# All loops of a hybrid block written out, and six PSUM banks shared three and three in its decayed attention

## The reference, cut to what matters

```python
x = x + mamba_block(_layernorm(x))        # stage "m"
x = x + local_attention_ffn(_layernorm(x))  # stage "t0", 2 layers
x = x + decayed_attention(_layernorm(x))  # stage "a"
x = x + local_attention_ffn(_layernorm(x))  # stage "t1", the same 2 layers
```

```python
qkv = x @ Wqkv_w.T + Wqkv_b                  # 16 heads of 8 columns
scores = einsum('bhsd,bhtd->bhst', q, k) / sqrt(8)
decay = exp(-abs(distance_decay[0]) * abs(s - t))
attn = softmax(scores * decay, axis=-1)      # over all 512 positions
out = einsum('bhst,bhtd->bhsd', attn, v)
return out @ out_w.T + out_b
```

## Time and profile before

| | |
|---|---|
| median of 3 runs (lowest to highest) | 2450.01 us (2449.64 to 2451.04) |
| profiled execution, its own time | 2449.7 us |
| its span | 2447.9 us |
| share of the span: PE, PEld, DVE, ACT, POOL | 90%, 61%, 67%, 61%, 69% |
| mean granted clock of PE | 0.96 of full speed |
| stage m | about 0 to 300 us |
| stage t0: local attention, feed-forward, for each layer | 300 to 605, 605 to 678; 678 to 965, 965 to 1045 |
| stage a, the decayed attention | 1045 to 1700 |
| stage t1, as t0 | 1700 to 2005, 2005 to 2080; 2080 to 2370, 2370 to 2448 |

### The profile page before, as it was taken

How to read it: one execution, slowest core, us unless ns; L and a number is a source line. 1 busy time by engine, 2 the same in 40 slices (tenths; PEclk the granted TensorE clock), 3 DMA queues, 4 the chain that set the end, 5 groups by cost and what they waited for, 6 DMA issues and landing times.

```text
span 2447.9 us, 60289 instructions
## 1 busy us (share of the span) xinstructions
PE 2202.7 (90%) x19744; PEld 1500.7 (61%) x19760; DVE 1628.1 (67%) x3905; ACT 1487.5 (61%) x4130; POOL 1679.2 (69%) x1712
## 2 busy tenths in 40 slices
PE   6998799998989998949998889998999979999989
PEld 4776467775657775525555555554677755677755
DVE  5777578875567775636665566666788755677755
ACT  3555378886378886325554455554788853788853
POOL 6777699884188884247665667665899831888842
PEclk8999899999999998979999999999999999999999
DMA  4000011121111111121101110110111211111111
GB/s 108 1 0 1 6 39 31 27 46 28 41 43 36 36 34 26 36 61 53 43 21 41 52 46 20 38 52 17 29 37 28 46 23 46 41 36 33 35 28 49
DMA packets 121250, 86.69 MB, mean 35 GB/s; under 512 B 85560, under 2 KB 102160, under 8 KB 118800
## 3 DMA queue, kind: packets, MB, share of 16 engines
q1 hardware_dynamic: 119248, 82.70, 14.1%
q10 hardware_dynamic: 1856, 2.23, 0.3%
HBM read 30.38 MB, written 8.39 MB: 16 GB/s over the span
## 4 chain that ended last, share of the span: by engine, by line
PE 50%; DVE 12%; POOL 9%; issue 8%; DMA 5%; SPq 3%; ACT 1%; DVEq 0%; POOLq 0%
PE bank L1170 8%; POOL store L1010 6%; PE bank L519 6%; PE bank L638 5%; PE bank L1161 4%; PE bank L1181 4%; DMA store<-parts 4%; PE bank L553 3%; PE bank L566 3%; PE bank L592 3%; PE bank L647 3%; PE bank L533 3%; DVE store L842 2%; POOL store L1019 2%; DVE store L847 2%
## 5 line engine op out<-in xcount | busy, mean ns | idle before, releaser
L1398 POOL TENSOR_SCALAR store<-store 128x512 f32<-128x512 f32 x512 | 349.8, 697 | 217.9 <-DVE store L1315 216.2
L1272 ACT ACTIVATE store<-bank 128x512 f32<-128x512 f32 x512 | 285.9, 604 | 316.4 <-PE bank L1170 315.6
L1315 DVE CUSTOM_DVE_ANT_0 store<-bank,store 128x512 f32<-128x512 f32 x512 | 340.2, 689 | 189.4 <-PE bank L1161 118.9
L730 ACT ACTIVATE store<-bank,store 128x128 f32<-128x128 f32 x1024 | 364.2, 378 | 68.6 <-DVE store L860 68.5
L1010 POOL TENSOR_TENSOR store<-store 128x16 f32<-128x16 f32 x128 | 372.6, 2911 | 26.4 <-DVE store L856 26.4
L1004 POOL TENSOR_TENSOR store<-store 128x512 f32<-128x512 f32 x256 | 321.2, 1276 | 83.3 <-DVE store L847 82.0
L1170 PEld LDWEIGHTS bank<-store 128*128 128x128 f32 x2048 | 252.4, 147 | 136.3 <-ACT store L1272 78.3
L1170 PE MATMUL bank<-store 128*128 128x128 f32 x2048 | 309.7, 285 | 0.0
L519 PE MATMUL bank<-store 128*128 128x512 f32 x512 | 268.8, 612 | 8.5 <-DVE store L835 7.0
L1019 POOL TENSOR_TENSOR store<-store 128x512 f32<-128x512 f32 x256 | 261.6, 1043 | 17.4 <-POOL store L1010 11.4
L1161 PE MATMUL bank<-store 72*128 72x512 bf16 x512 | 186.6, 397 | 86.1 <-DMA store<-parts 46.8
(11 more groups left out here) (199 smaller groups left out, 4457.7 us busy)
## 6 DMA issues: line engine op xcount, KB each, us to landing
store<-store SPq DMA_DIRECT2D x256, 128.0 KB, 2.3
store<-parts SPq DMA_DIRECT2D x96, 192.0 KB
parts<-store SPq DMA_DIRECT2D x16, 384.0 KB, 2.5
store<-store SPq DMA_DIRECT2D x128, 32.0 KB
store<-store SPq DMA_DIRECT2D x128, 31.8 KB
store<-store SPq DMA_DIRECT2D x32, 127.0 KB
store<-in_L_ffn_wqkv_dram SPq DMA_DIRECT2D x4, 768.0 KB, 4.5
out_dram<-store SPq DMA_DIRECT2D x8, 256.0 KB, 2.6
```

The lines of the kernel that those rows point to most:

```text
L730: last = nc.scalar.activation(prob[:, e, b, :], bank[3 + e][:, b * P:(b + 1) * P], ACT.Exp, bias=nmax[:, e, b:b + 1], accum_out=psums[:, h ...
L1272: nc.scalar.activation(AT[:, h % 4, c, :], bank[2 + c][:, :], ACT.Exp, scale=-1.0).then_inc(aexp_done, 1)
L1315: nc.vector.tensor_tensor_reduce(out=S[:, h % 4, t, :], in0=bank[t % 2][:, :], in1=decay[:, off:off + L], scale=1.0, scalar=-3.0e38, op0=A ...
L1398: nc.gpsimd.tensor_scalar(s_, s_, -1.0, amax[:, h % 4, t:t + 1], ALU.mult, ALU.add).then_inc(shifted_done, 1)
```

## The change

Every `with engine.Fori(...)` becomes a Python `for`, so the instructions of all 8 sequences stand in the program one after another, and every value that a semaphore must reach is a constant. In the decayed attention the six banks for scores and transposes are shared three and three. Banks 0 to 2 take the scores and banks 3 to 5 the transposes, each by a running number taken modulo 3, and since 64 is not a multiple of 3 the banks of a tile differ from sequence to sequence. A score waits for the scaling of the score three before it, and a turn for the exponential of the turn three before it. The start values of the two semaphores (`credits`) move by the same numbers, and with them the counts that `weigh` and `subtract_max` wait for, which stand for the same events as before. SCORES and LEAD stay, and so does the order of the work on each engine.

```diff
@@ -322,6 +322,7 @@
         COMBOS = 2 * PARTS
+        SCORE_BANKS, TURN_BANKS = 3, 3
...
-                   (scaled_done, 2), (aexp_done, TPS), (at_done, 16), (ao_ready, 1), (av_out, TPS),
+                   (scaled_done, SCORE_BANKS), (aexp_done, TURN_BANKS), (at_done, 16), (ao_ready, 1), (av_out, TPS),
...
-                with pe.Fori(1, B - 1) as s:
+                for s in range(1, B - 1):
                     attention_sequence(q0 + s, True, True)
...
-                    with pool.Fori(0, B - 1) as s:
+                    for s in range(0, B - 1):
                         attention_sequence(s, q0 + s, True)
...
-            with sp.Fori(0, B - 1) as q:
+            for q in range(0, B - 1):
...
                 pe.wait_ge(scaled_done, 64 * q + k + 1)
-                nc.tensor.matmul(bank[t % 2][:, :], QC[0:COMBO, h, t * P:(t + 1) * P], KC[0:COMBO, h, :],
+                nc.tensor.matmul(bank[(64 * q + k) % SCORE_BANKS][:, :], QC[0:COMBO, h, t * P:(t + 1) * P], KC[0:COMBO, h, :],
                                  start=True, stop=True).then_inc(score_done, 1)
...
                 pe.wait_ge(aexp_done, 64 * q + 4 * h + c + 1)
                 for t in range(TPS):
-                    last = nc.tensor.transpose(bank[2 + c][:, t * P:(t + 1) * P], S[:, h % 4, t, c * P:(c + 1) * P], ident)
+                    last = nc.tensor.transpose(bank[SCORE_BANKS + (64 * q + 4 * h + c) % TURN_BANKS][:, t * P:(t + 1) * P], S[:, h % 4, t, c * P:(c + 1) * P], ident)
...
-                pe.wait_ge(aexp_done, 64 * q + 16 * g + c + 17)
+                pe.wait_ge(aexp_done, 64 * q + 16 * g + c + 13 + TURN_BANKS)
...
-            with pe.Fori(1, B - 1) as q:
+            for q in range(1, B - 1):
                 sequence(q, True, True)
...
-                    nc.scalar.activation(AT[:, h % 4, c, :], bank[2 + c][:, :], ACT.Exp, scale=-1.0).then_inc(aexp_done, 1)
+                    nc.scalar.activation(AT[:, h % 4, c, :], bank[SCORE_BANKS + (64 * q + 4 * h + c) % TURN_BANKS][:, :], ACT.Exp, scale=-1.0).then_inc(aexp_done, 1)
...
-                nc.vector.tensor_tensor_reduce(out=S[:, h % 4, t, :], in0=bank[t % 2][:, :], in1=decay[:, off:off + L],
+                nc.vector.tensor_tensor_reduce(out=S[:, h % 4, t, :], in0=bank[(64 * q + 4 * h + t) % SCORE_BANKS][:, :], in1=decay[:, off:off + L],
...
-            with dve.Fori(1, B - 2) as q:
+            for q in range(1, B - 2):
                 sequence(q, True, True, True)
...
-                pool.wait_ge(scaled_done, 64 * q + 4 * h + t + 3)
+                pool.wait_ge(scaled_done, 64 * q + 4 * h + t + 1 + SCORE_BANKS)
...
-            with pe.Fori(0, (B - 4) // 2) as s:
+            for s in range(0, (B - 4) // 2):
                 sequence(2 * s + 1, 1, True, True, True)
                 sequence(2 * s + 2, 0, True, True, True)
```

More of the change, by code:

```diff
@@ L481, in transformer_sp @@
                     load_ff(sp, l)
-                with sp.Fori(0, B - 1) as s:
+                for s in range(0, B - 1):
                     if l == 0:
@@ L690, in transformer_pe @@
                 ff_round(q0 + 1, 1, False, True)
-                with pe.Fori(2, B - 2, 2) as s:
+                for s in range(2, B - 2, 2):
                     ff_round(q0 + s, 0, False, True)
@@ L785, in transformer_act @@
                 attention_sequence(q0, False, True)
-                with act.Fori(1, B - 1) as s:
+                for s in range(1, B - 1):
                     attention_sequence(q0 + s, True, True)
@@ L794, in transformer_act @@
                 ff_affine(q0, 0)
-                with act.Fori(0, B - 2, 2) as s:
+                for s in range(0, B - 2, 2):
                     ff_round(q0 + s, 0, True)
@@ L968, in transformer_dve @@
                 if l == 0:
-                    with dve.Fori(1, B - 2) as s:
+                    for s in range(1, B - 2):
                         attention_sequence(s, q0 + s, True, True, True)
@@ L972, in transformer_dve @@
                 else:
-                    with dve.Fori(1, B - 1) as s:
+                    for s in range(1, B - 1):
                         attention_sequence(s, q0 + s, True, True)
@@ L982, in transformer_dve @@
                 ff_round(1, q0 + 1, 1, False, True, last_layer)
-                with dve.Fori(2, B - 2, 2) as s:
+                for s in range(2, B - 2, 2):
                     ff_round(s, q0 + s, 0, False, True, last_layer)
@@ L1066, in transformer_pool @@
                 if l == 0:
-                    with pool.Fori(0, B - 2) as s:
+                    for s in range(0, B - 2):
                         attention_sequence(s, q0 + s, True, True)
@@ L1076, in transformer_pool @@
                 meet(pool, l * 2 + meets + 1)
-                with pool.Fori(0, B - 2, 2) as s:
+                for s in range(0, B - 2, 2):
                     for odd in range(2):
@@ L1301, in decayed_act @@
             sequence(0, False, True)
-            with act.Fori(1, B - 1) as q:
+            for q in range(1, B - 1):
                 sequence(q, True, True)
@@ L1418, in decayed_pool @@
                     split(0, t, step)
-            with pool.Fori(0, B - 2) as q:
+            for q in range(0, B - 2):
                 sequence(q, True, True)
@@ L1735, in mamba_act @@
             sequence(0, 0, False, True, True)
-            with act.Fori(0, (B - 4) // 2) as s:
+            for s in range(0, (B - 4) // 2):
                 sequence(2 * s + 1, 1, True, True, True)
@@ L1865, in mamba_dve @@
             sequence(0, 0, False, True, True, True)
-            with dve.Fori(0, (B - 4) // 2) as s:
+            for s in range(0, (B - 4) // 2):
                 sequence(2 * s + 1, 1, True, True, True, True)
@@ L1978, in mamba_pool @@
             sequence(0, 0, False, True, True, True)
-            with pool.Fori(0, (B - 4) // 2) as s:
+            for s in range(0, (B - 4) // 2):
                 sequence(2 * s + 1, 1, True, True, True, True)
```

## The result

| | before | after |
|---|---|---|
| median of the runs (lowest to highest) | 2450.53 us (2449.64 to 2457.97) | 2412.91 us (2412.38 to 2414.04) |
| ratio, 95% interval | | 0.9841, 0.9821 to 0.986 |
| profiled execution, its span | 2449.7, 2447.9 | 2412.38, 2410.6 |

37.6 us are gained where 42.0 were forecast, and the direction and the range held. Lines of the kernel after are one higher: L1162 is a score, L1171 a turn, L1316 DVE's scaling.

What follows compares the result with a forecast made beforehand. PE was taken to bound the kernel, with whatever opens its gaps. Decayed-attention loops 24.1, banks 10, local attention 7.3 and mamba 0.6 sum to 42.0 us off 2449.7, giving 2408 us, range 2396 to 2428.

Steps and rivals of the forecast that it cites:

- The branch of DVE: Decayed attention, four sequence boundaries where DVE branches back: written out, they become like the other two, 24.1 us gained.
- the fourth rival: Decayed attention: the boundary stall belongs to the sequence's end, not DVE's branch; 24.1 us stay away, 2432 us; chance 0.05.
- The banks: Decayed attention: a third score bank removes PE's waits for DVE's scaling, 10 us net gain, at most 14.
- The landing: Next sequence's DMA arrives a fixed 31.4 us after POOL's first split; PE's savings inside that, 9.2 us, are lost.
- the second rival: Decayed attention: with three banks the transposes become the bound, turns waiting for ACT's exponentials; 2434 us, chance 0.07.
- the clock: Decayed attention: a longer DMA wait and low PE clock cost 0.5 us in each of six sequences, 3 us.
- the first rival: Decayed attention: the banks give nothing, as the DMA landing paces every sequence and the clock takes savings; 2418 us, chance 0.20.
- The local attention: Local attention: written-out loops remove POOL's 0.22 us wait in looped blocks; 7.3 us gained, bounds 4 and 12.
- Mamba: Mamba stage: 31.07 us across the branch against 30.74 written out, about 0.6 us gained over five sequences.
- The third rival: Local attention loops: written-out code is never on hand, each pass pays a 3.07 us fetch; 2482 us, chance 0.06.
- the sign named for being wrong: Issue stalls inside the local attention, named among the observations that would show the forecast wrong.
- The range: Whole kernel: the forecast's own range was 2397 to 2421 us; the stated range was 2396 to 2428.

Runs made afterwards that it cites:

- x3_dve_loop: The kernel before, with only DVE's loop of the decayed attention written out: 2424.98 us, ratio 0.9887.
- x1_loops: The kernel after, all loops written out, but with the banks of before, two for scores and four for transposes: 2419.2 us, ratio 0.9863 to before.
- x5_split_24: x4_split with the banks of before, two for scores and four for transposes: 2392.84 us, ratio 0.976 to before.
- x8_pool_loops: x2_stage_a with POOL's loops of the local attention and feed-forward written out as well: 2420.55 us, ratio 0.9864 to before.
- x2_stage_a: The kernel after, with hardware loops kept everywhere but in the decayed attention: 2419.05 us, ratio 0.9873 to before.
- x4_split: The kernel after, with POOL's six steps splitting the next sequence's q and k at heads 8 and 9, not 8 to 10: 2365.13 us, ratio 0.9645 to before.
- x6_before_split: The kernel before, loops and banks unchanged, with only the split of q and k moved to heads 8 and 9: 2436.65 us, ratio 0.9937.

## Why the prediction was right, and where it was not

**The branch of DVE, 24.1 us: right.** The whole argument was that six boundaries are alike but for DVE's branch. x3_dve_loop changes that alone and makes them alike, and x1_loops puts the decayed stage's loops at 23.6 us. The two values, 26.9 and 23.6, lie apart by no more than the stage scatters. With this the fourth rival falls. Of the five engines' branches only this one counted, as the boundary 5 to 6 had said. The prediction names 3.07 us for the stall; that is the shortest of the four, and the sum does not rest on it.

**The banks, 10 us: the mechanism right, the size right in part by luck.** In the stage 8.9 us remain, against x1_loops. The waits for DVE gave 21.3 where 23.2 were booked (x1_loops has 21.8, after 0.5). The landing took back 8.9, booked at 9.2. No turn waits for ACT, booked at 1, so the second rival falls at three banks. What I did not foresee is a turn that waits for POOL's subtraction, 3.2 us in six places, since a score that starts sooner does not make POOL faster. That leaves 9.2, so nearly nothing seems left for the clock, for which I had booked 3: "I take 0.5 us in each of six sequences". But PE's busy time shows two effects that cancel. In the five steady sequences together it is 345.92 us in x1_loops and 345.94 in after, though the clock is 0.98 there and 0.96 here. At one clock three banks make it shorter: 68.54 us in the one steady sequence that after ran at 0.98, against 69.15 to 69.25 in those of x1_loops, and 0.74 less at 1.00 (x5_split_24). The lower clock takes that back. Of the clock I had about the right size, and the shorter busy time I did not have at all.

The medians leave 6.3, less than the 8.9. Behind the stage after loses 1.7 us against x1_loops (749.8 from the last division to the end of the span, against 748.1), in stretches that have the same instructions; the passage to t1 runs at 0.50 and 0.65 in after (above) and at 1.00 in x1_loops. With stage times of 582.31 to 587.67 us for one and the same code, neither 8.9 nor the 10 is known to a microsecond. The five steady sequences gained 2.3 us together. So the first rival, at 0.20, came near for the steady sequences and was wrong for the first one and the last two.

**The local attention, 7.3 us: second layers right, first layers half.** A sequence without norms gains 0.30 us (34.12 to 33.82, forecast 0.28). One with norms gains 0.16, because only part of the two waits of 0.22 reaches PE there (x8_pool_loops); the bounds of that part reached upwards, and the value lay below them. And t0's and t1's layers together gained only 0.48 + 1.52 + 0.97 + 1.45 = 4.4 us between their first and last inverse norms. The products of sequence and gain would give 7 x 0.30 x 2 + 6 x 0.16 x 2 = 6.1. The rest went in the first sequence of a layer, where the second and the third inverse norms stand 8.79, 8.73, 8.26 and 8.71 us apart against 8.24, 8.26, 8.21 and 8.21 before. This is the clock and not the loops. The 6 us around the second inverse norms of t0's first layer, before and after:

```profile
312.57:318.57 6.00, 5.97 (x46) 2.79 (x44) 1.04 (x2) 2.10 (x5) 5.92 (x5) 0.74 0.04 10
```
```profile
310.75:316.75 6.00, 6.00 (x46) 2.90 (x44) 0.48 (x1) 2.19 (x4) 5.92 (x5) 0.64 0.01 3
```

In after the clock is 0.64 to 0.66 at the three places with 8.71 to 8.79 us and 0.72 at the one with 8.26. The same holds across kernels: x2_stage_a, with its loops, has 9.07 us at 0.59 in t1, and x4_split, without any, 8.20 at 0.72 in t0 and 7.71 at 0.84 in t1. Why the clock stands lower at one time than at another is open.

**Mamba, 0.6 us:** 1.05 by the rows. The prediction does not say how 0.6 follows from the 0.33 us of the earlier trace rows, and those two rows stand at 0.95 and 1.00 of the clock. As x8_pool_loops and x2_stage_a show, this stage moves by up to 10 us with nothing changed in it, so neither number means much.

**The third rival, code that is never on hand:** fell. With every loop written out, DVE has no issue gap over 1.4 us at the boundaries, and the local attention is faster. One issue gap of DVE in after looks like the sign named for being wrong, 3.06 us at 1670.34 in t1's first block. It stands where PE's four products take 3.75 us at half clock instead of 1.95, and x6_before_split, with all its loops, has it too (3.03), so it is not the code. The rule of the Trainium skill named in the prediction ("Runtime: NRT & Kernel Launch", section "Instruction fetch mechanics"), that straight code is fetched ahead, agrees with these traces.

**The range.** The lower gain of the forecast's own range was given as 21 + 4 + 4, though the text sets the banks' lower bound at 0; one of the two fours has no source. Nothing hangs on it.

**Open:** in the kernels with the decayed attention's loops written out on all engines the landing comes 0.3 to 1.0 us later behind the first split, in the mean of seven (31.08 us before, 31.12 in x3_dve_loop; 31.41 in x1_loops, 31.53 in x8_pool_loops, 31.74 in x2_stage_a, 32.11 after). It could be the larger instruction traffic or scatter: single ones run from 29.3 to 33.4, and the last three kernels are the same in this stage.

## What to carry to other kernels

Writing out loops pays where a branch is on the path: find two boundaries in the profile that differ only in who branches, and change that one engine. A change of buffers is worth what the next fixed latency lets through: 6.3 us with the landing late and 27.7 with it early, by the same edit. So move the pacing transfer first, and measure the rest again.

## What the hardware showed that was not expected

- DVE's stall behind its branch went with what else was under way: 3.07 us with 33 packets of SP's queue during it, 5.01 with 80, and 4.91 to 5.34 with 105 to 109. An experiment that moves a transfer under a branch can lose there part of what it gains elsewhere, as x6_before_split did.
- Short waits of PE cost more than their length. With x4's split 30.4 us of such waits went, and the stage became 45.1 us shorter; the clock of a steady sequence rose from 0.95 to 1.00.
- Where the clock falls is not repeated from one kernel to the next in stages that are the same: the passage to t1 ran at 0.50 in one profile and at 1.00 in another (1.8 us), and mamba at 0.95 and at 0.98 in the rows above (10.9 us in all, from the start to t0). The decayed attention of one and the same code took 582.31 to 587.67 us. Differences of 2 us in an untouched stage should not be given a cause.
